# Maxima of an attention item in two halves, keyed scores 16 steps behind, and no prologue in a 12-stage decoder kernel

## The chip, the cores and the metric

One NeuronCore of a Trainium2 chip runs the whole program in one launch. The metric is the device time of that launch in microseconds (us). The engines are TensorE (PE in the profile, its weight loads PEld), VectorE (DVE), ScalarE (ACT), GpSimd (POOL) and SyncE (SP), which here only issues DMAs.

## The reference

Four decoder layers run over `x` of 8 sequences x 256 tokens x 128 features in float32. Each layer has three parts, each with a layer norm before it and a residual after it: `x = x + attn(ln(x))`, `x = x + xattn(ln(x), ctx)`, `x = x + ffn(ln(x))`. What matters here are the five attention parts that share one routine:

- L0a and L1a: causal self-attention of 16 heads of width 8, with rotary positions on queries and keys;
- L0x and L1x: cross-attention to `ctx` with a mask; L0x also multiplies each probability by a given matrix ("group prob") after the softmax;
- L3x: plain cross-attention.

Each computes `softmax(q k^T / sqrt(8)) v` per head and a projection. L0f, L1f and L2f are mixtures of 8 experts with a routed token each; L2a, L2x, L3a and L3f are other parts, which the change leaves as they are.

## The kernel before

`program` calls `start`, then one function per stage. `attention(core, sts)` is called three times: for the pair L0a and L0x, for L1a and L1x, and for L3x alone. Every stage ends with a barrier of all engines (`end_pass`).

**`start`** (from line 2087) loads the weights, `ctx`, `x`, fills the constant rows of the images in DRAM, zeroes `sorted_in` (8.8 MB of DRAM that L0f needs) from GpSimd's queue, turns `ctx`, and issues the expert weights of L0f. It is a block of its own, so that nothing of the attention group starts before all engines have left it.

**Items and slots.** An item is one sequence of one stage, so a pair has 16 items and L3x has 8. Item i's work is put at fixed slots: step number `16 * i + offset`. Each engine's program is written by one loop over the slots (`for n in SLOTS`), and within a slot in the fixed order of the `if` blocks. The queues are in order, so the offsets decide what stands behind what. Offsets modulo 16 say which slot of the running item j a step of another item falls in:

- statistics, aggregate, variance (DVE), Ln and Exp (ACT) and the normalisation (POOL, `normalise`, lines 486 to 497) of item j+3 are at slots 0, 1, 2, 3, 4 and 5;
- the transposition of x is at slot 10, the projections K and Q of item j+2 at slots 14 and 4, and V of item j at slot 8;
- `cut` (line 378) splits a float32 matrix into three bfloat16 parts. For item j+2 it stands on POOL at slot 1 for k and slot 7 for q (the first two items on DVE). A rotary item needs five operations (lines 383 to 389), another two (388 and 389);
- SP writes the parts to an image in DRAM and reads them back in another layout (`parts_out`, `stack_in`), which gives the tiles `Kst` and `Qm`;
- `scores` (line 653), one unit per slot, 16 per item, is followed by `row_max` on DVE (line 875). PE runs at most two units ahead of DVE;
- after all 16 maxima of an item `cut_max` (POOL, lines 505 to 508, slot 16), `turn_max` (PE, line 608, slot 18), a copy (ACT, slot 19) and two DMAs (SP, line 463, slot 20) put the maxima as extra rows into `Qm`;
- `keyed_scores` (line 673, with line 675 or 678 for masks) makes the scores once more, transposed and with the maximum subtracted, TLAG = 24 slots behind `scores`. ACT takes the exponential (line 769). For L0x the product with the group matrix is on POOL in 5 of 8 units (line 525) and on DVE in the others, at slot 25 on. `times_v` (line 703) takes four units at a time, at slots 2, 6, 10 and 14;
- choosing heads (`SEL`), dividing, transposing (`AT`, line 626), projecting (`Y`) and adding to X are at 45, 49 and 55. `Xb`, the residual with the bias, is made on POOL at offset 45 (slot 13, line 556).

At the start of each attention call DVE zeroes `Qm` (lines 924 and 925) and `vaug` (line 927) between the steps of the first item. In the pair L1a and L1x SP issues the experts' weights (2 x 2 MB, line 1402) before all else.

## Time and profile before

| | us |
|---|---|
| median of 3 runs (lowest to highest) | 1810.36 (1806.36 to 1817.83) |
| the profiled execution, its own time | 1812.71 |
| span of its profile | 1810.9 |
| first attention group, first statistics to last residual | 56.9 to 435.6 |
| second group | 561.6 to 901.2 |
| third group | 1483.8 to 1662.3 |

The time of the profiled execution is 1.8 us above its span. The page gives busy time by engine and by slices of the span, the timeline gives instructions in order with the idle time before them and who ended it, and the answer for a tile gives first and last start of the instructions that use it. The clock column PEclk is 1.0 at 2.4 GHz and 0.5 at 1.2 GHz. The three attention groups take 897 us of the 1811, and the block in front of the first takes 56.9.

### The profile page before, as it was taken

Reading aid. Unit: us, or ns where it says so; the run is one execution under the profiler, and the core shown is the slowest. Engines: PE = TensorE matmul, PEld = TensorE weight load, DVE = VectorE, ACT = ScalarE, POOL = GpSimd, SP = SyncE. Lnnn points to the kernel's source line nnn. Section 1 sums busy time; section 2 is a strip of 40 time slices with the busy share of each in tenths; the row PEclk is TensorE's granted clock in tenths of the full one; section 3 lists DMA queues with packets and bytes.
Section 4 is the critical chain, followed back from the end, with each engine's and each line's share of the span. In section 5 each row is a group of like instructions: output and inputs, shape, how many; then the busy total and the mean of one; then the engine's idle time right before and its main releaser. Section 6 shows DMA issues by size and latency. Waiting matters only on the chain. (4 is left out here: it accounts for less than half of the span.)

```text
span 1810.9 us, 30796 instructions
## 1 busy us (share of the span) xinstructions
PE 1278.4 (71%) x9105; PEld 805.9 (45%) x9105; DVE 1026.2 (57%) x4304; ACT 604.7 (33%) x1441; POOL 556.3 (31%) x931
## 2 busy tenths in 40 slices
PE   0289999995392799999739255645677765996686
PEld 0146555553291456555329133435644432553332
DVE  0478787764776777777267522456533346773432
ACT  0025554442040255556404112102232322664221
POOL 1256368873341544463034000004300003411000
PEclk9879999998596799999959655876878886998798
DMA  9633443300114334443011300001200004320000
GB/s 251 205 118 113 137 147 116 115 23 14 35 53 177 119 113 121 143 133 112 4 39 56 143 0 0 13 31 52 67 8 0 0 32 141 112 86 3 0 0 23
DMA packets 134311, 138.28 MB, mean 76 GB/s; under 512 B 11328, under 2 KB 106176, under 8 KB 133136
## 3 DMA queue, kind: packets, MB, share of 16 engines
q1 hardware_dynamic: 128208, 119.79, 21.5%
q0 software_dynamic: 5952, 16.68, 3.3%
q8 instruction: 70, 1.15, 0.3%
q14 instruction: 81, 0.66, 0.1%
HBM read 84.10 MB, written 49.70 MB: 74 GB/s over the span
## 5 line engine op out<-in xcount | busy, mean ns | idle before, releaser
L769 ACT ACTIVATE L0a_Pr<-PS 128x512 f32<-128x512 f32 (+1 forms) x256 | 137.1, 547 | 159.3 <-PE PS L678 94.2
L769 ACT ACTIVATE L1a_Pr<-PS 128x512 f32<-128x512 f32 (+1 forms) x256 | 136.2, 548 | 122.6 <-PE PS L675 65.0
L525 POOL TENSOR_TENSOR L0a_PG<-L0a_Pr,L0a_G 128x512 f32<-128x512 f32 x80 | 106.6, 1336 | 29.1 <-ACT L0a_Pr L769 17.1
L875 DVE CUSTOM_DVE_ANT_0 L1a_junk<-PS,L1a_neg 128x256 bf16<-128x256 f32 x256 | 94.7, 420 | 35.1 <-PE PS L653 34.9
L653 PE MATMUL PS<-L0a_Kst,L0a_Qm 128*128 128x256 bf16 (+1 forms) x512 | 94.7, 271 | 11.6 <-DVE L0a_mx L875 10.7
L653 PE MATMUL PS<-L1a_Kst,L1a_Qm 128*128 128x256 bf16 (+1 forms) x512 | 94.2, 270 | 11.6 <-DVE L1a_mx L875 10.6
L878 DVE TENSOR_REDUCE L3x_mx<-PS 128x2 f32<-128x512 f32 x128 | 83.7, 686 | 31.9 <-PE PS L653 31.5
L673 PE MATMUL PS<-L1a_Qm,L1a_Kst 128*128 128x512 bf16 (+1 forms) x256 | 91.0, 356 | 9.2 <-DMA L1a_Qm<-L1a_mT 6.0
L875 DVE CUSTOM_DVE_ANT_0 L1a_junk<-PS,causal_q 128x128 bf16<-128x128 f32 (+1 forms) x256 | 78.3, 352 | 30.2 <-PE PS L653 29.5
L875 DVE CUSTOM_DVE_ANT_0 L0a_junk<-PS,causal_q 128x128 bf16<-128x128 f32 (+1 forms) x256 | 78.3, 352 | 30.1 <-PE PS L653 29.4
L673 PE MATMUL PS<-L0a_Qm,L0a_Kst 128*128 128x512 bf16 (+1 forms) x256 | 90.8, 355 | 5.7 <-DMA L0a_Qm<-L0a_mT 2.9
L875 DVE CUSTOM_DVE_ANT_0 L0a_junk<-PS,L0a_neg 128x256 bf16<-128x256 f32 x192 | 72.8, 418 | 38.8 <-PE PS L653 38.2
L769 ACT ACTIVATE L3x_Pr<-PS 128x512 f32<-128x512 f32 x128 | 73.5, 603 | 46.2 <-PE PS L673 45.8
L675 PE MATMUL PS<-neg_k,ident_b 128*128 128x256 bf16 x256 | 70.1, 274 | 0.0
L653 PEld LDWEIGHTS PS<-L0a_Kst,L0a_Qm 128*128 128x128 bf16 x512 | 44.0, 102 | 57.0 <-DVE L0a_mx L875 32.4
L653 PEld LDWEIGHTS PS<-L1a_Kst,L1a_Qm 128*128 128x128 bf16 x512 | 43.7, 102 | 56.9 <-DVE L1a_mx L875 31.7
L1063 POOL MEMSET L2f_ends<- 128x4 f32 x2 | 0.1, 101 | 204.7 <-POOLq L1571 204.7
L703 PE MATMUL PS<-L1a_Pr,L1a_vaug 128*32 128x256 f32 (+1 forms) x1024 | 61.7, 358 | 0.2 <-ACT L1a_Pr L769 0.2
L653 PE MATMUL PS<-L3x_Kst,L3x_Qm 128*128 128x256 bf16 x256 | 51.9, 288 | 7.5 <-DVE L3x_mx L878 4.7
L673 PE MATMUL PS<-L3x_Qm,L3x_Kst 128*128 128x512 bf16 x128 | 48.8, 389 | 9.7 <-ACT L3x_Pr L769 5.1
L678 PE MATMUL PS<-L0a_neg,ident_b 128*128 128x512 bf16 x128 | 48.8, 381 | 0.0
L678 PE MATMUL PS<-L1a_neg,ident_b 128*128 128x512 bf16 x128 | 48.5, 379 | 0.0
(727 smaller groups left out, 3291.8 us busy)
## 6 DMA issues: line engine op xcount, KB each, us to landing
ffn_w_<-L_ffn SPq DMA_DIRECT2D x6, 2048.0 KB, 11.9
sorted_in<-zeros POOLq DMA_DIRECT2D x2, 4386.0 KB, 42.8
L0a_Kst<-k_image SPq DMA_DIRECT2D x64, 128.0 KB
L0a_Qm<-q_image SPq DMA_DIRECT2D x64, 128.0 KB
L1a_Kst<-k_image SPq DMA_DIRECT2D x64, 128.0 KB
L1a_Qm<-q_image SPq DMA_DIRECT2D x64, 128.0 KB
L3x_Kst<-k_image SPq DMA_DIRECT2D x32, 128.0 KB
L3x_Qm<-q_image SPq DMA_DIRECT2D x32, 128.0 KB
```

Of the source, the lines that this page charges most:

```text
L525: g.tensor_tensor(PG[:, V_ % GATED_RING, :].rearrange("p (h q) -> p h q", h=2), Pr[:, V_ % RING, :].rearrange("p (h q) -> p h q", h=2), G[ ...
L653: ins = mm(PS[:, bank, par * nk:(par + 1) * nk], Qm[:, buf, par, hp, tt * P:(tt + 1) * P], Kst[:, buf, hp, 0:nk], start=(par == 0), stop=T ...
L673: ins = mm(o, Kst[:, buf, hp, kt * P:(kt + 1) * P], Qm[:, buf, :, hp, q0:S], start=True, stop=True, **free)
L675: ins = mm(o[:, :, 0:P], core.ident_b[:, :], core.neg_k[:, :].unsqueeze(1).broadcast_to([P, 2, P]), start=False, stop=True, **free)
L678: ins = mm(o, core.ident_b[:, :], neg[:, buf, 1, kt].unsqueeze(1).broadcast_to([P, 2, S]), start=False, stop=True, **free)
L703: ins = mm(o, vaug[:, buf, half, kt, 4 * g + j, :], src[:, par * nq:(par + 1) * nq], start=(kt == 0 and half == 0), stop=True, **free)
L769: a(Pr[:, V_ % RING, 0:2 * nq], PS[:, T_BANK + v % 2, 0:2 * nq], ACT.Exp, scale=SCALE)\
L875: ins = v.tensor_tensor_reduce(junk[:, tt, par, 0:nk], scored[:, par], off, 1.0, LOWEST, ALU.add, ALU.max, mx[:, i % 2, tt, par, hp:hp + 1])
L878: ins = v.tensor_reduce(mx[:, i % 2, tt, :, hp:hp + 1], scored, AX, ALU.max)
L1063: nc.gpsimd.memset(ends[k][:, 0:E // 2], 0.0).then_inc(s["pads"], 1)
```

## The change

1. `start` is removed. Its loads are issued by SP at the head of the first attention call (`first_loads`): the part of `x` for the first two sequences, common weights, L0a's weights, the rest of `x`, the constant rows, `ctx`. The transposition of `ctx` is at slot -12 of the first group, the constant casts on DVE at slot -36.
2. `sorted_in` is zeroed in 8 parts, one per item at slot 5 on POOL's queue, and the experts' weights of L0f and L1f come one expert per item at slot 5 on SP's queue, where they were issued before the group's first item.
3. `Qm` and `vaug` live through the whole program and are zeroed once, at the start.
4. The statistics of the first three items of a group are made early (`LEAD`), with three buffers, and their K and Q steps are drawn together by 4 and 8 slots. Of item 0, the k stack is read back two slots ahead of the q stack.
5. The maxima of an item are handled in two halves: `cut_max` at slots 8 and 16, `turn_max` at 9 and 17, the copy at 10 and 18, the DMAs at 11 and 19. Operations and DMAs are twice as many at half the size.
6. TLAG is 16 where it was 24; V, SEL, AT, Y, XB and GATE_IN move with it (XB to slot 5, SEL to 5, AT to 8, Y to 11), and the two PSUM banks of these steps are dealt out anew.

```diff
-        self.zeros = sb("zeros", [P, 2 * (D + 1)])
+        self.zeros = sb("zeros", [P, D + 1])
+        self.Qm = sb("Qm", [P, DEPTH, 2, HP, S], BF16)
+        self.vaug = sb("vaug", [P, DEPTH, 2, TS, HP, 32])
...
-    EARLY = 2
+    RUNS = 3
...
     STATS, AGGR, VAR, LN, EXP, NORM = -48, -47, -46, -45, -44, -43
-    XT, K, Q, V, MT, SEL, AT, Y = -38, -34, -28, 8, 18, 45, 49, 55
-    K_CUT, Q_CUT, K_OUT, Q_OUT, MAX_CUT, MAX_IN = -31, -25, -27, -21, 16, 20
-    STACK_IN, FIRST_STACK_IN = (-13, -7), -20
-    MASK_IN, NEG, GATE_IN, XB = -23, -7, 4, 45
-    TLAG = 24
+    XT, K, Q, V, SEL, AT, Y = -38, -34, -28, 7, 37, 40, 43
+    MAX_CUT, MT, MAX_IN = (8, 16), (9, 17), (11, 19)
+    K_CUT, Q_CUT, K_OUT, Q_OUT = -31, -25, -27, -21
+    STACK_IN, FIRST_STACK_IN = (-13, -7), {"k": -22, "q": -20}
+    MASK_IN, NEG, GATE_IN, XB, FFN_IN, ZERO_IN = -23, -7, -4, 37, 5, 5
+    CONSTS, CTX = -36, -12
+    TLAG = 16
     PV_LAG = TLAG + 6
     SLOTS = range(STATS, PER * (N - 1) + Y + 2)
-    f_bank = lambda off: F_BANK + (off // 2) % 2
+    FILLED = {XT: 0, K: 0, SEL: 0, AT: 0, Q: 1, V: 1, Y: 1, MT[0]: 1, MT[1]: 1}
+    f_bank = lambda off: F_BANK + FILLED[off]
+    LEAD = {off: (0, 11, 20) for off in (STATS, AGGR, VAR, LN, EXP, NORM, XT, XT + 1)}
+    LEAD.update({off: (0, 4, 8) for k in (K, Q) for off in range(k, k + 8)})
+    def slot_of(i, off):
+        return PER * i + off - (LEAD[off][i] if i < 3 and off in LEAD else 0)
     def at(n, off):
-        i, r = divmod(n - off, PER)
-        return i if r == 0 and 0 <= i < N else None
+        return next((i for i in range(N) if slot_of(i, off) == n), None)
+    def before(n, off):
+        return sum(1 for i in range(N) if slot_of(i, off) < n)
...
-    def stack_slot(i, half):
-        return PER * i + (FIRST_STACK_IN if i < DEPTH else STACK_IN[half])
+    def stack_slot(i, half, what):
+        if i >= DEPTH:
+            return PER * i + STACK_IN[half]
+        return FIRST_STACK_IN[what] if i == 0 else PER * i + FIRST_STACK_IN["q"] - LEAD[Q][i]
+    cut_on_dve = lambda i, what: i == 0 or i == 1 and what == "k"
...
-        mrest = sb("mrest", [P, TS, 2, HP])
-        mpart = sb("mpart", [P, TS, 2, DH, HP], BF16)
-        mT = sb("mT", [P, S], BF16)
+        mrest = sb("mrest", [P, TS, 2, HP // 2])
+        mpart = sb("mpart", [P, TS, 2, 2, DH, HP // 2], BF16)
+        mT = sb("mT", [64, 2, S], BF16)
...
+                if first:
+                    first_loads(core, sp)
                 load_next_weights(core, sp)
-                if sts[0] == "L1a":
-                    load_ffn(core, sp, "L1")
-                sp.wait_ge(s["image_set"], 16 * 6)
...
+                    for half in range(2):
+                        i = at(n, MAX_IN[half])
                         if i is not None:
-                            if i >= DEPTH:
-                                sp.wait_ge(s["st_psum"], PER * (i - DEPTH) + 8 * (half + 1))
-                            if i == 0:
-                                sp.wait_ge(s["setup"], set_up)
-                            stack_in(i, half, "k")
-                            stack_in(i, half, "q")
-                    i = at(n, MAX_IN)
-                    if i is not None:
-                        sp.wait_ge(s["mT_ready"], i + 1)
-                        for par in range(2):
-                            sp.dma_start(Qm[64 * par + 56:64 * par + 64, i % DEPTH, par].rearrange("c p t -> c (p t)"),
-                                         mT[64 * par:64 * par + 64, :])\
-                                .then_inc(s[f"max_in{i % 2}"], 16)
+                            sp.wait_ge(s["mT_ready"], 2 * i + half + 1)
+                            for par in range(2):
+                                to = Qm[64 * par + 56:64 * par + 64, i % DEPTH, par, 4 * half:4 * half + 4]
+                                sp.dma_start(to.rearrange("c p t -> c (p t)"), mT[32 * par:32 * par + 32, half, :])\
+                                    .then_inc(s[f"max_in{i % 2}_{half}"], 16)
+                    i = at(n, FFN_IN)
+                    if i is not None and i < E and second:
+                        if first and i == 0:
+                            sp.wait_ge(s["ctx_psum"], 4)
+                        load_expert(core, sp, sts[0][:2], i)
...
+                if first:
+                    still = core.ffn[1][:, 0:S].bitcast(BF16).rearrange("p (k t) -> p k t", k=2)
+                    for k in range(2):
+                        g.memset(still[:, k, :], -float(k)).then_inc(s["still_set"], 1)
+                    g.memset(vaug[:, :, :, :, :, :], 0.0).then_inc(s["setup"], 1)
+                    g.memset(core.zeros[:, :], 0.0).then_inc(s["consts"], 1)
+                g.memset(mpart[:, :, :, :, NMAX:DH, :], 0.0).then_inc(s["setup"], 1)
...
-                def cut_max(i):
-                    pool.wait_ge(s["s_max"], PER * (i + 1))
+                def cut_max(i, half):
+                    pool.wait_ge(s["s_max"], PER * i + 8 * (half + 1))
                     if i > 0:
-                        pool.wait_ge(s["mT_psum"], i)
-                    hi, mid, lo = (mpart[:, :, :, k, :] for k in range(NMAX))
-                    top = mx[:, i % 2]
+                        pool.wait_ge(s["mT_psum"], 2 * (i - 1) + half + 1)
+                    hi, mid, lo = (mpart[:, :, half, :, k, :] for k in range(NMAX))
+                    top = mx[:, i % 2, :, :, 4 * half:4 * half + 4]
...
+                    for half in range(2):
+                        i = at(n, MAX_CUT[half])
+                        if i is not None:
+                            cut_max(i, half)
+                    i = at(n, ZERO_IN)
+                    if first and i is not None and i < ZERO_PARTS:
+                        if i == 0:
+                            pool.wait_ge(s["consts"], 2)
+                        some = SORTED_ROWS // ZERO_PARTS
+                        pool.dma_start(core.dram["sorted_in"][i * some:(i + 1) * some].rearrange("(p b) d -> p b d", p=P),
+                                       core.zeros[:, :].unsqueeze(1).broadcast_to([P, some // P, D + 1]))\
+                            .then_inc(s["rows_zero"], 16)
...
-                def turn_max(i, bank, n):
-                    pe.wait_ge(s["m_parts"], i + 1)
+                def turn_max(i, half, bank, n):
+                    pe.wait_ge(s["m_parts"], 2 * i + half + 1)
                     bank_empty(n, bank)
+                    if first and i == 0:
+                        pe.wait_ge(s["consts"], 2)
                     for t in range(TS):
-                        ins = tr(PS[:, bank, t * 64:t * 64 + 64].bitcast(BF16),
-                                 mpart[:, t].rearrange("p r c h -> p (r c h)"), core.ident_b[:, :])
+                        ins = tr(PS[0:64, bank, t * 64:t * 64 + 64].bitcast(BF16),
+                                 mpart[:, t, half].rearrange("p r c h -> p (r c h)"), core.ident_b[:, :])
...
-                    if v == 0:
-                        pe.wait_ge(s[f"max_in{i % 2}"], 32 * (i // 2 + 1))
+                    if v % 8 == 0:
+                        pe.wait_ge(s[f"max_in{i % 2}_{v // 8}"], 32 * (i // 2 + 1))
+                    if first and i == 0 and v == 0:
+                        pe.wait_ge(s["ctx_done"], 4)
...
+                if first:
+                    v.memset(Qm[0:64, :, 1], 0.0).then_inc(s["setup"], 1)
+                    v.memset(Qm[64:P, :, 0], 0.0).then_inc(s["setup"], 1)
...
-                    if n == VAR + 1:
-                        v.memset(Qm[0:64, :, 1], 0.0)
-                        v.memset(Qm[64:P, :, 0], 0.0).then_inc(s["setup"], 1)
-                    if n == K + 3:
-                        v.memset(vaug[:, :, :, :, :, :], 0.0).then_inc(s["setup"], 1)
...
-def load_ffn(core, eng, ly):
+def load_expert(core, eng, ly, e):
     for n in (0, 1):
-        eng.dma_start(core.ffn[n][:, :], core.dram[f"{ly}_ffn{n + 1}"]).then_inc(core.sem[f"ffn_w{ly[1]}"], 16)
+        cols = slice(e * F, (e + 1) * F)
+        eng.dma_start(core.ffn[n][:, cols], core.dram[f"{ly}_ffn{n + 1}"][:, cols]).then_inc(core.sem[f"ffn_w{ly[1]}"], 16)
...
+def first_loads(core, sp):
+    s = core.sem
+    tokens = lambda n: core.dram[n].rearrange("(t p) d -> p t d", p=P)
+    near = NSEQ * TS
+    sp.dma_start(core.X[:, 0:near, :], tokens("x")[:, 0:near, :]).then_inc(s["x_in"], 16)
+    sp.dma_start(core.W[:, :], core.dram["small_common"]).then_inc(s["w_in"], 16)
+    sp.dma_start(core.stage_W[0][:, 0:width(WEIGHTS[STAGES[0]])], core.dram[f"small_{STAGES[0]}"]).then_inc(s["first_w"], 16)
+    sp.dma_start(core.X[:, near:, :], tokens("x")[:, near:, :]).then_inc(s["x_rest"], 16)
+    still = core.ffn[1][:, 0:S].bitcast(BF16).rearrange("p (k t) -> p k t", k=2)
+    sp.wait_ge(s["still_set"], 2)
+    for k in range(2):
+        still_rows = lambda n: core.dram[f"{n}_image"][k, 6:8].rearrange("s r t -> r s t")
+        sp.dma_start(still_rows("k"), still[:, :, :]).then_inc(s["image_set"], 16)
+        for slot in range(2):
+            sp.dma_start(still_rows("q")[:, slot:slot + 1, :], still[:, 0:1, :]).then_inc(s["image_set"], 16)
+    sp.dma_start(core.ffn[0][:, 0:B * S].rearrange("p (t d) -> p t d", d=D), tokens("ctx")).then_inc(s["ctx_tok"], 16)
```

## Rows read from the trace of the kernel before

**Rows 1.** The page, busy time, share of the span and instructions of each engine.
```profile
PE 1278.4 (71%) x9105; PEld 805.9 (45%) x9105; DVE 1026.2 (57%) x4304; ACT 604.7 (33%) x1441; POOL 556.3 (31%) x931
```

**Rows 2.** Timeline, first 60 us: start, length, engine, line, tiles, idle before and releaser.
```profile
1.88 3.74 POOL L2121 DMA_DIRECT2D sorted_in<-zeros  x2 [0.32 <-POOL zeros L2117]
...
49.48 0.81 SPq L1402 DMA_DIRECT2D ffn_w_<-L_ffn  x2
...
56.93 0.49 DVE L909 BATCH_NORM_STATS2 L0a_st<-X 128x6 f32<-128x128 f32 x2 [50.79 <-PEq L2093]
```

**Rows 3.** By tile Qm, three groups: ns min/median/max, first to last start in us.
```profile
L653 PE MATMUL PS<-L0a_Kst,L0a_Qm x512: 216/273/421, 89.0 to 397.0; 128*128 128x256 bf16 x128, 128*128 128x128 bf16 x43
L673 PE MATMUL PS<-L0a_Qm,L0a_Kst x256: 272/379/634, 112.8 to 425.9; 128*128 128x512 bf16 x96, 128*128 128x256 bf16 x32
...
L653 PE MATMUL PS<-L1a_Kst,L1a_Qm x512: 216/273/421, 593.6 to 871.2; 128*128 128x256 bf16 x128, 128*128 128x128 bf16 x43
L673 PE MATMUL PS<-L1a_Qm,L1a_Kst x256: 272/379/634, 617.5 to 893.6; 128*128 128x512 bf16 x96, 128*128 128x256 bf16 x32
...
L653 PE MATMUL PS<-L3x_Kst,L3x_Qm x256: 269/273/421, 1510.0 to 1635.5; 128*128 128x256 bf16 x128
L673 PE MATMUL PS<-L3x_Qm,L3x_Kst x128: 379/379/634, 1532.4 to 1655.0; 128*128 128x512 bf16 x128
```

**Rows 4.** Timeline, starts of the second and third attention group.
```profile
561.57 0.49 DVE L909 BATCH_NORM_STATS2 L1a_st<-X 128x6 f32<-128x128 f32 x2 [3.10 <-PEq L1039]
...
563.11 2.62 DVE L924 MEMSET L1a_Qm<- 64x3072 uint32 x1 [0.57 <-issue]
...
571.34 2.62 DVE L927 MEMSET L1a_vaug<- 128x3072 f32 x1 [0.59 <-issue]
...
580.37 1.36 SPq L422 DMA_DIRECT2D L1a_Kst<-k_image  x2
...
1483.76 0.49 DVE L909 BATCH_NORM_STATS2 L3x_st<-X 128x6 f32<-128x128 f32 x2 [2.40 <-PEq L1694]
```

**Rows 5.** Timeline of POOL in one item of L0a.
```profile
159.06 0.19 POOL L488 TENSOR_TENSOR L0a_nsq<-L0a_r 128x2 f32<-128x2 f32 x1 [0.95 <-ACT L0a_r L787]
...
160.20 1.57 POOL L495 TENSOR_SCALAR L0a_xn<-X,L0a_mv,L0a_rstd 128x128 f32<-128x128 f32 x2
161.74 0.73 POOL L383 TENSOR_TENSOR L0a_qrot<-L0a_qrot 128x256 f32<-128x256 f32 x1
...
164.22 0.67 POOL L389 TENSOR_TENSOR L0a_qpart<-L0a_qrest,L0a_qpart 128x256 bf16<-128x256 f32 x1
164.85 0.86 POOL L556 TENSOR_TENSOR L0a_Xb<-X,stage_W 128x128 f32<-128x128 f32 x2
170.70 0.21 POOL L505 CAST L0a_mpart<-L0a_mx 128x32 bf16<-128x32 f32 x1 [4.98 <-DVE L0a_mx L875]
...
171.59 0.24 POOL L508 TENSOR_TENSOR L0a_mpart<-L0a_mrest,L0a_mpart 128x32 bf16<-128x32 f32 x1
```

**Rows 6.** Timeline of PE in the same item.
```profile
153.05 0.28 PE L653 MATMUL PS<-L0a_Kst,L0a_Qm 128*128 128x128 bf16 x2
...
162.67 0.27 PE L675 MATMUL PS<-neg_k,ident_b 128*128 128x256 bf16 x1
...
171.90 0.41 PE L626 MATMUL PS<-W,L0a_A 128*128 128x128 f32 x2 [0.49 <-DVE L0a_A L958]
```

**Rows 7.** Timeline of POOL and PE in two items of L0x.
```profile
283.06 0.21 POOL L505 CAST L0a_mpart<-L0a_mx 128x32 bf16<-128x32 f32 x1
...
309.58 0.21 POOL L505 CAST L0a_mpart<-L0a_mx 128x32 bf16<-128x32 f32 x1
...
323.39 0.64 PE L703 MATMUL PS<-L0a_PG,L0a_vaug 128*32 128x256 f32 x8 [2.19 <-POOL L0a_PG L525]
```

**Rows 8.** PE in L1x after a wait; then windows: busy us, PEclk, DMA share, GB/s.
```profile
735.69 0.61 PE L673 MATMUL PS<-L1a_Qm,L1a_Kst 128*128 128x512 bf16 x1 [3.16 <-DMA L1a_Qm<-L1a_mT]
...
735.00:740.00 5.00, 4.31 (x34) 2.90 (x35) 1.89 (x12) 1.79 (x3) 2.65 (x2) 0.66 0.42 113
```

More of the change, by code:

```diff
@@ L296, in attention @@
     S_BANK, T_BANK, O_BANK, F_BANK = 0, 2, 4, 6
+    first = core.at == 0
     any_masked = any(st in MASKED for st in sts)
@@ L450, in _ @@
                     for half in range(2):
-                        i = next((j for j in range(N) if stack_slot(j, half) == n), None)
-                        if i is not None:
-                            if i >= DEPTH:
-                                sp.wait_ge(s["st_psum"], PER * (i - DEPTH) + 8 * (half + 1))
-                            if i == 0:
-                                sp.wait_ge(s["setup"], set_up)
-                            stack_in(i, half, "k")
-                            stack_in(i, half, "q")
@@ L713, in _ @@
                 for n in SLOTS:
+                    if first and n == CTX:
+                        pe.wait_ge(s["ctx_tok"], 16)
+                        for k in range(4):
+                            for t in range(4):
+                                ins = tr(PS[:, T_BANK + k, t * P:(t + 1) * P], core.ffn[0][:, (4 * k + t) * D:(4 * k + t + 1) * D],
+                                         w("ident"))
+                            ins.then_inc(s["ctx_psum"], 1)
                     i, u = unit(n, 0)
@@ L734, in _ @@
                         project_v(i, f_bank(V), n)
-                    i = at(n, MT)
-                    if i is not None:
-                        turn_max(i, f_bank(MT), n)
+                    for half in range(2):
+                        i = at(n, MT[half])
+                        if i is not None:
+                            turn_max(i, half, f_bank(MT[half]), n)
                     i = at(n, SEL)
@@ L770, in exponentials @@
                         .then_inc(s["p_ready"], 1)
+                if first:
+                    nc.scalar.preload_act_table_set("natural_log_exp_and_others")
                 for n in SLOTS:
+                    if first and n == CTX + 1:
+                        for k in range(4):
+                            act_copy(core, act, core.ctxT[:, k * 512:(k + 1) * 512], PS[:, T_BANK + k, :], s["ctx_psum"], k + 1,
+                                     s["ctx_done"])
                     i, v = unit(n, TLAG)
@@ L799, in _ @@
                         first_part(i, "q", f_bank(Q))
[L800 to L805 removed]
+                    for half in range(2):
+                        i = at(n, MT[half] + 1)
+                        if i is not None:
+                            act.wait_ge(s["mT_psum"], 2 * i + half + 1)
+                            if i > 0:
+                                act.wait_ge(s[f"max_in{(i - 1) % 2}_{half}"], 32 * ((i - 1) // 2 + 1))
+                            a(mT[:, half, :], PS[0:64, f_bank(MT[half]), 0:P].bitcast(BF16), ACT.Copy).then_inc(s["mT_ready"], 1)
                     i = at(n, AT + 1)
@@ L850, in take_v @@
                         dve.wait_ge(s["pv_done"], 4 * (i - DEPTH + 1))
+                    if first and i == 0:
+                        dve.wait_ge(s["setup"], set_up)
                     halves = vaug[:, buf].rearrange("p a t h r -> p a (t h) r")
@@ L1428, in _ @@
                 load_next_weights(core, sp)
-                load_ffn(core, sp, "L2")
+                for e in range(E):
+                    load_expert(core, sp, "L2", e)
                 end_pass_sync(core, sp, "channel_attention")
@@ L2166, in program @@
         core = Core(nc, ctx, dram)
-        start(core)
         for core.at, st in enumerate(STAGES):
```

192 lines of the change are left out of this document (75 added, 117 removed).

## The prediction

> **What bounds the kernel now.** I read the page first, then the timeline of the first 100 us, the answers for the tile Qm, and then the timelines of POOL and PE inside single items. PE is the busiest engine [rows 1]. The start is idle time: DVE waits 50.79 us for the barrier at the end of the first block and begins at 56.93, while DMAs fill the queues and the experts' weights are issued at 49.48 [rows 2]. Scores begin at 89.0, 593.6 and 1510.0 in the three groups, keyed scores 24 slots later, and they end 28.9, 22.4 and 19.5 us after the last scores [rows 3]. Inside an item of L0a slot 0 of PE starts at 153.05 and the last matmul of slot 9 at 162.67. Slot 1 of the next item comes at 171.9 less a wait of 0.49 [rows 6], so an item is some 16.8 us. PE has few gaps in it, so what makes PE wait in its queue costs time.
>
> **The start (step 1, 2).** Before, scores start at 89.0 [rows 3]. After, DVE first has two memsets of Qm, 2.62 us each [rows 4], and its statistics start at about 6.6. The chain from statistics to scores is bounded by group two: 561.57 to 593.6, 32.0 us, with three memsets of 2.62 in DVE's queue [rows 3, 4]. Without them and with the next items' statistics out of the way, what ends last is SP. The k parts are ready some 10.5 us after the statistics (14.3 before, less three memsets and the steps between, plus a rotation of another item). Two image writes of three DMAs and eight reads of stacks at 0.6 to 0.7 us each (the row has two in 1.36) and two landings of about 2 us follow, one pair after the other because k is read back before q is written. That is 24 us. In the first group the image DMAs stand behind about 4 MB of loads, so I add 1 us: 6.6 + 24 = 31. **Gain 58 us.** The bounds are 47 (chain as in group two, 6.6 + 32 + 3 of queueing) and 62. The wait for x's second part on DVE, the constant casts and the turning of ctx lie in gaps of that chain. If the loads came late, all of it would move.
>
> **Starts of groups two and three (steps 2 to 4).** 32.0 becomes 24, so 8 us. Group three has 1483.76 to 1510.0, 26.2 us, with the short cuts [rows 3, 4]; there SP's chain gives 22, so 4 us. **Gain 12**, bounds 0 and 22 (all memsets of both).
>
> **The lag (step 6).** Eight slots of keyed scores alone leave each tail. The rows give 28.9 / 24 = 1.20, 22.4 / 24 = 0.93 and 19.5 / 24 = 0.81 us each [rows 3], so 9.6 + 7.5 + 6.5 = **24 us gain**. In the head eight slots then have both kinds of scores. The head's 24 slots last 23.8, 23.9 and 22.4 us [rows 3], 1.0 a slot, and a full slot of L0a is 16.8 / 16 = 1.05, so I take that at nothing; the bound is 8 x 0.3 in each group, 7 us.
>
> **The halves (step 5) and POOL's order.** This is the price. Four operations of `cut_max` take 170.70 to 171.8, 1.1 us, and at half the width I take the same, since small operations are 0.21 and 0.24 long [rows 5]. The first half stands at slot 8, behind all that POOL has at slots 5 and 7: `normalise` 159.06 to 161.77 (2.7 us), now Xb (0.86, moved from slot 13 to slot 5), and the q cut 161.74 to 164.89 (3.15) [rows 5]. `normalise` can't start before the Exp of slot 4, for which POOL waited 0.95 in that row. So the parts of half 0 are ready at 159.06 + 2.7 + 0.86 + 3.15 + 1.1 = 166.9. PE asks for them at the end of slot 9, 162.8 [rows 6]. PE stands 4.1 us, and behind it stand scores, keyed scores, the products with V and x's transposition of slot 10, and so DVE and ACT. Before, the request was at slot 18, two slots after the cut, and POOL was idle for 4.98 us ahead of it [rows 5].
> - L0a and L1a, running items 2 to 5: 4.1 less about 0.5 that the caught-up DVE gives back, 3.6. Item 1 has no Xb: 2.7. Items 6 and 7 have the short q cut (1.1): 1.6. Item 0 has only the normalisation: 0. That is 14.4 + 2.7 + 3.2 = 20 a group, **40 us**.
> - Half 1 is asked for in slot 1, about 0.6 us before it is ready, where PE now waits 0.49 for the A of the AT step [rows 6]; these cancel.
> - L0x: POOL also has the gate products, and PE already waits 2.19 us at slot 10 for that of slot 8 [rows 7]. An item with normalisation lasts 309.58 - 283.06 = 26.5 us [rows 7]. In front of PE's slot 10 come Xb (1.3 beside the gates, by my reading of the row's 0.86 as the lower bound), the cut (1.1), the scores of slot 10 (0.65) and, since half 1 stands behind the gate product of slot 0, some 2 us at slot 1. I take 5.6 for each of items 9 to 12, 1.5 for item 8 and 3 for each of 13 to 15: **33 us**, bounds 12 (only the cuts, 16 x 1.1 less what slack takes) and 45.
> - L1x and L3x have no gates and the short cut: 0 to 2.1 for each of 10 items, I take 1, less the 3.16 us wait for a maxima DMA [rows 8], which now has one slot more: **7 us**.
>
> **Small edits.** The eight zeroing parts move to POOL's slot 5. Two DMAs took 3.74 us to issue [rows 2], so a part is 0.9 (by rows) to 1.9 (by DMA), and 0.95 of idle time stands ahead of the normalisation [rows 5]; nothing, bound 8. If that idle time is gone, it adds to the stall of the same item. The doubled maxima DMAs are 0.65 us each on SP, which has room. The memsets of vaug and the small buffers on POOL at the start end before the first normalisation. Expert weights come 0.5 MB an item beside image DMAs: nothing, bound 4.
>
> **The clock.** After the 3.16 us wait the next 5 us ran at 0.66 of the full clock [rows 8]. At half clock for some 3.4 us of it, 1.7 us are lost. Of 14 stalls of about 4 us or more (5 and 5 in L0a and L1a, 4 in L0x) I let a third lose it: **8 us**. "TensorE: Matmul & The Clock Gate" of the Trainium skill (Part 1) says that the full clock is not a boost but what activity gives and idleness takes away, which speaks against this change. By it nearly each such stall would cost the clock, and the sum would be 16 us higher. The row agrees in kind: it shows the half level (1.2 GHz) entering the mean right after a wait.
>
> **The sum** against the profiled execution's 1812.7: gains 58 + 12 + 24 = 94; prices 40 + 33 + 7 + 8 = 88. That is 1807 in that execution, which lies 2.3 us over the median of the runs shown, so 1805.
>
> **Rivals.**
> 1. *The stalls are mostly taken up* (0.32). For it: PE's matmuls are pipelined, each stall lets ACT and DVE catch up, an item of 16.8 us has some 2 us of small gaps, and POOL's chain could start earlier than the row shows. Against it: POOL's queue is in order and its 7.8 us between Exp and parts are row values. At a third of the price (27 us and no clock): 1810 - 94 + 27 = 1743; at two thirds 1770. I put this case at 1765.
> 2. *The clock falls after nearly each stall* (0.22, slower). Place: slots 10 to 13 behind each wait for the first half. Price: 1.7 us for each of 14 long stalls and 8 shorter ones, 37 instead of 8, and with it PE gives back nothing of the caught-up DVE (0.5 x 12 = 6): 1805 + 29 + 6 = 1840. It decides if the mean clock of L0a's middle windows, 1.0 before, falls under about 0.9.
> 3. *The start is not as early* (0.08): the loads queue as before and scores begin at 45 to 50 instead of 31; 1820 to 1824, with the rest as forecast. Related: the change of order does nothing to the barrier's 50 us, which the diff excludes.
>
> **How the numbers follow.** Forecast 0.38, rivals 0.32, 0.22 and 0.08. 1% of 1810.36 is 18 us, the least that a measurement of this kernel tells from no change. The forecast's own range is 1785 to 1825: of its 0.38 some 0.08 is faster, 0.28 the same, 0.02 slower. Rival 1 is faster with nearly all of its 0.32, rival 2 slower with 0.19, the same with 0.01 and faster with 0.02 (if the start gives 62 and the tails more), rival 3 is 0.05 the same and 0.03 slower. So faster 0.42, same 0.34, slower 0.24. Cases of both signs hold much of the chance; the range reaches from two thirds absorbed to the clock rival: 1743 to 1842.
>
> **What would show it.** First scores at 29 to 34 us confirm the start; 24 us from the first statistics of group two to its scores the second term. In L0a, PE's wait ahead of line 608's successor for POOL's parts should be 3.5 to 4.5 us in items 1 to 5, with POOL busy from `normalise` to the cut without a gap, and the item at 20 us. L0x items should last 29 to 32 us. Scores to last keyed scores in the tail: 19 us in L0x and 15 in L1x. I am wrong if POOL reaches `cut_max` of slot 8 before PE ends slot 9, or if an item of L0a stays below 17.5 us; then the time is that of rival 1 or lower.

## The result and the profile after

The changed kernel takes 1959.6 us (median of 4 runs, 1950.0 to 1964.1) against 1811.1 for the kernel before (4 runs, 1806.4 to 1817.8): a ratio of 1.081, 95% interval 1.076 to 1.086, so 148 us slower. The profiled execution took 1949.99 us with a span of 1948.2; the sum below is made in the two spans, 1810.9 and 1948.2.

First the page of the changed kernel: busy time of the engines, the granted clock in 40 slices, and three groups with their idle time and what ended it.

```profile
PE 1329.0 (68%) x9185; PEld 822.5 (42%) x9185; DVE 1011.3 (52%) x4285; ACT 623.7 (32%) x1481; POOL 596.4 (31%) x1110
...
PEclk8688899999587699888895955586869985999698
...
L724 PE MATMUL PS<-Qm,L1a_Kst 128*128 128x512 bf16 (+1 forms) x256 | 98.8, 386 | 51.0 <-DMA Qm<-L1a_mT 49.5
L724 PE MATMUL PS<-Qm,L0a_Kst 128*128 128x512 bf16 (+1 forms) x256 | 96.8, 378 | 44.5 <-DMA Qm<-L0a_mT 43.1
```

Against [rows 1] PE has 50 us more busy time for nearly the same products (80 small matmuls more, of the halves): they ran at the half clock more often. But the two last lines are the news. Keyed scores (line 724) wait 92.6 us for the DMA that brings the maxima into Qm. On the page of the kernel before, the same wait was 8.9 us, and the prediction used one case of it, 3.16 us [rows 8]:

```profile
L673 PE MATMUL PS<-L1a_Qm,L1a_Kst 128*128 128x512 bf16 (+1 forms) x256 | 91.0, 356 | 9.2 <-DMA L1a_Qm<-L1a_mT 6.0
...
L673 PE MATMUL PS<-L0a_Qm,L0a_Kst 128*128 128x512 bf16 (+1 forms) x256 | 90.8, 355 | 5.7 <-DMA L0a_Qm<-L0a_mT 2.9
```

The tile Qm shows how the stretches moved, in the changed kernel:

```profile
L702 PE MATMUL PS<-L0a_Kst,Qm x512: 219/273/421, 33.0 to 453.6; 128*128 128x256 bf16 x128, 128*128 128x128 bf16 x43
...
L702 PE MATMUL PS<-L1a_Kst,Qm x512: 219/273/421, 638.7 to 1002.8; 128*128 128x256 bf16 x128, 128*128 128x128 bf16 x43
...
L724 PE MATMUL PS<-Qm,L0a_Kst x256: 272/379/634, 74.2 to 476.5; 128*128 128x512 bf16 x96, 128*128 128x256 bf16 x32
...
L724 PE MATMUL PS<-Qm,L1a_Kst x256: 272/379/634, 665.8 to 1017.9; 128*128 128x512 bf16 x96, 128*128 128x256 bf16 x32
...
L702 PE MATMUL PS<-L3x_Kst,Qm x256: 269/273/421, 1633.2 to 1778.7; 128*128 128x256 bf16 x128
...
L724 PE MATMUL PS<-Qm,L3x_Kst x128: 379/379/634, 1659.2 to 1792.1; 128*128 128x512 bf16 x128
```

With the first statistics and the last write of X of each group, read in the same way, the two spans split like this (us):

| stretch | before | after | difference | forecast |
|---|---|---|---|---|
| start to first scores | 89.0 | 33.0 | -56 | -58 |
| group 1, first scores to last X | 346.5 | 454.3 | +108 | about +50 |
| group 2, statistics to scores | 32.0 | 24.5 | -8 | -8 |
| group 2, first scores to last X | 307.6 | 386.3 | +79 | about +20 |
| group 3, statistics to scores | 26.2 | 22.8 | -3 | -4 |
| group 3, first scores to last X | 152.3 | 166.2 | +14 | about -5 |
| everything between and behind | 857.3 | 861.1 | +4 | 0 |

The starts came as forecast. The tails, last scores to last keyed scores, went from 28.9, 22.4 and 19.5 [rows 3] to 22.9, 15.1 and 13.4: 19 us of the 24. Nearly all that was missed lies inside the items. From the last keyed scores of group 2 to the first scores of group 3, work which the runs below hardly alter, it takes 607 to 622 us over the profiled executions of all kernels, so a few us mean nothing there.

**POOL's order, as predicted.** An item of L0a of the changed kernel in the timeline, the same stretch as [rows 5, 6] (start, length, engine, line); POOL first:

```profile
171.28 0.86 POOL L599 TENSOR_TENSOR L0a_Xb<-X,stage_W 128x128 f32<-128x128 f32 x2
172.11 0.72 POOL L403 TENSOR_TENSOR L0a_qrot<-L0a_qrot 128x256 f32<-128x256 f32 x1
...
174.58 0.67 POOL L409 TENSOR_TENSOR L0a_qpart<-L0a_qrest,L0a_qpart 128x256 bf16<-128x256 f32 x1
175.19 0.20 POOL L539 CAST L0a_mpart<-L0a_mx 128x16 bf16<-128x16 f32 x1
...
176.03 0.22 POOL L542 TENSOR_TENSOR L0a_mpart<-L0a_mrest,L0a_mpart 128x16 bf16<-128x16 f32 x1
```

PE in the same stretch:

```profile
172.58 0.38 PE L724 MATMUL PS<-Qm,L0a_Kst 128*128 128x512 bf16 x1
172.80 0.27 PE L726 MATMUL PS<-neg_k,ident_b 128*128 128x256 bf16 x1
176.30 0.42 PE L657 MATMUL PS<-ident_b,L0a_mpart 128*64 128x128 bf16 x2 [3.23 <-POOL L0a_mpart L542]
176.66 0.39 PE L702 MATMUL PS<-L0a_Kst,Qm 128*128 128x128 bf16 x2
176.84 0.63 PE L724 MATMUL PS<-Qm,L0a_Kst 128*128 128x512 bf16 x1
```

Xb, the q cut and `cut_max` follow one another without a gap, and PE stands 3.23 us for the parts. The same matmul takes 0.38 us ahead of the wait and 0.63 behind it: PE is at the half clock. The granted clock is 0.97 in 172.0 to 176.3 us and 0.57 in 176.3 to 180.0. In L1a the same wait is 1.94 us an item, and it is enough: the granted clock is 1.00 in 694.0 to 696.4, the wait ends at 698.38, and in 698.4 to 700.0 the clock is 0.50 and in 700 to 702 it is 0.57.

**SP's order, not predicted.** The same view of POOL in an item of L1x:

```profile
898.89 0.22 POOL L542 TENSOR_TENSOR L1a_mpart<-L1a_mrest,L1a_mpart 128x16 bf16<-128x16 f32 x1
899.20 3.93 POOL L551 TENSOR_SCALAR L1a_neg<-L1a_msk 128x512 bf16<-128x512 int32 x2
```

And of SP's queue beside it, then PE's next keyed scores:

```profile
892.54 1.46 SPq L433 DMA_DIRECT2D k_image<-L1a_kpart  x3
903.15 0.37 SPq L458 DMA_DIRECT2D L1a_msk<-mask1q  x1
...
904.14 1.29 SPq L441 DMA_DIRECT2D L1a_Kst<-k_image  x2
...
908.33 1.45 SPq L485 DMA_DIRECT2D Qm<-L1a_mT  x2
...
912.12 0.61 PE L724 MATMUL PS<-Qm,L1a_Kst 128*128 128x512 bf16 x1 [5.00 <-DMA Qm<-L1a_mT]
```

At slot 9 SP asks for the next masks, for which POOL must have used the last ones. POOL does so from 899.20 to 903.13, and SP stands from 894 to 903.15. Behind it, in SP's queue, stand two stack reads, the q image writes and, since the change, the maxima DMA of slot 11. It used to be at slot 20, which is slot 4 of the next item and 11 slots behind the mask wait; now it is 2 slots behind. It is issued at 908.33, and keyed scores begin at 912.1 after a wait of 5.00 us.

**Landings.** The DMA view of 105 to 235 us: queues with packets, MB and share; transfers with their count, size and us from issue to landing. First the kernel before:

```profile
q1 hardware_dynamic: 19672, 16.10, 41.0%
...
k_image<-L0a_kpart SPq DMA_DIRECT2D x8, 64.0 KB, 1.8
```

The changed kernel, with the two loads that moved in:

```profile
q1 hardware_dynamic: 16378, 15.23, 46.1%
q0 software_dynamic: 1575, 6.11, 31.0%
...
sorted_in<-zeros POOLq DMA_DIRECT2D x5, 1096.5 KB, 13.7
...
ffn_w_<-L_ffn SPq DMA_DIRECT2D x10, 256.0 KB, 11.1
...
k_image<-L0a_kpart SPq DMA_DIRECT2D x5, 64.0 KB, 12.2
```

A transfer of 64 KB that landed in 1.8 us takes 12.2. It is one of the three that write a k image; the one of 192 KB went from 2.1 us to 2.9, the one of 128 KB from 2.1 to 9.8. In item 0 the first maxima DMA is ready at 47.9 (ACT's copy), issued from 63.9 because SP stands at the stacks of items 1 and 2, whose images land late, and PE waits 21.04 us for it, at the start of item 1.

### The profile page after: what moved, and what is told of

It reads as the page before. It is cut to its first block and busy times, and to the rows that moved or that the text cites. A ratio compares the mean times of both kernels' runs of the same rounds, so it can differ in the third digit from the quotient of the medians.

```text
span 1948.2 us, 31472 instructions
## 1 busy us (share of the span) xinstructions
PE 1329.0 (68%) x9185; PEld 822.5 (42%) x9185; DVE 1011.3 (52%) x4285; ACT 623.7 (32%) x1481; POOL 596.4 (31%) x1110
## 5 line engine op out<-in xcount | busy, mean ns | idle before, releaser
L724 PE MATMUL PS<-Qm,L1a_Kst 128*128 128x512 bf16 (+1 forms) x256 | 98.8, 386 | 51.0 <-DMA Qm<-L1a_mT 49.5
L724 PE MATMUL PS<-Qm,L0a_Kst 128*128 128x512 bf16 (+1 forms) x256 | 96.8, 378 | 44.5 <-DMA Qm<-L0a_mT 43.1
L702 PE MATMUL PS<-L1a_Kst,Qm 128*128 128x256 bf16 (+1 forms) x512 | 99.6, 283 | 10.0 <-DMA Qm<-q_image 5.8
L702 PE MATMUL PS<-L0a_Kst,Qm 128*128 128x256 bf16 (+1 forms) x512 | 98.1, 279 | 10.3 <-DMA Qm<-q_image 6.7
L726 PE MATMUL PS<-neg_k,ident_b 128*128 128x256 bf16 x256 | 75.4, 294 | 0.0
L702 PEld LDWEIGHTS PS<-L1a_Kst,Qm 128*128 128x128 bf16 x512 | 44.9, 105 | 54.3 <-issue 22.6
L754 PE MATMUL PS<-L1a_Pr,vaug 128*32 128x256 f32 (+1 forms) x1024 | 67.2, 385 | 0.7 <-ACT L1a_Pr L828 0.7
L702 PEld LDWEIGHTS PS<-L0a_Kst,Qm 128*128 128x128 bf16 x512 | 45.2, 105 | 51.1 <-issue 19.6
L702 PE MATMUL PS<-L3x_Kst,Qm 128*128 128x256 bf16 x256 | 53.3, 295 | 10.4 <-DVE L3x_mx L946 6.5
L724 PE MATMUL PS<-Qm,L3x_Kst 128*128 128x512 bf16 x128 | 49.4, 390 | 9.2 <-DMA Qm<-L3x_mT 7.3
L724 PEld LDWEIGHTS PS<-Qm,L1a_Kst 128*128 128x128 bf16 x256 | 26.7, 104 | 63.2 <-DMA Qm<-L1a_mT 51.9
L729 PE MATMUL PS<-L1a_neg,ident_b 128*128 128x512 bf16 x128 | 52.7, 412 | 0.0
```

Of the source, the lines that this page charges most:

```text
L702: ins = mm(PS[:, bank, par * nk:(par + 1) * nk], Qm[:, buf, par, hp, tt * P:(tt + 1) * P], Kst[:, buf, hp, 0:nk], start=(par == 0), stop=T ...
L724: ins = mm(o, Kst[:, buf, hp, kt * P:(kt + 1) * P], Qm[:, buf, :, hp, q0:S], start=True, stop=True, **free)
L726: ins = mm(o[:, :, 0:P], core.ident_b[:, :], core.neg_k[:, :].unsqueeze(1).broadcast_to([P, 2, P]), start=False, stop=True, **free)
L729: ins = mm(o, core.ident_b[:, :], neg[:, buf, 1, kt].unsqueeze(1).broadcast_to([P, 2, S]), start=False, stop=True, **free)
L754: ins = mm(o, vaug[:, buf, half, kt, 4 * g + j, :], src[:, par * nq:(par + 1) * nq], start=(kt == 0 and half == 0), stop=True, **free)
```

## The experiments

Three theories. **Q**: order in in-order queues, POOL's (cut behind q cut) and SP's (maxima DMA behind the mask wait). **D**: the zeroing parts and expert loads make short transfers land late. **C**: the clock and the short lag as such. An item is counted in its group: items 0 to 7 of group 1 are L0a's, 8 to 15 L0x's, and so for L1a and L1x. The first four go from the changed kernel.

```
e1:  MASK_IN  -23 -> -20
e2:  Q_CUT    -25 -> -24;   XB  37 -> 41
e3:  items 8..15 instead of 0..7 for FFN_IN and ZERO_IN (i -= B)
e4:  TLAG 16 -> 24;  V, SEL, AT, Y, GATE_IN, XB, banks as in the kernel before
     MAX_CUT, MT, MAX_IN = (14, 16), (16, 18), (18, 20)
```

**Masks asked for later (e1).**

> One number of the changed kernel is altered: SP asks for the next masks three slots later (slot -20 instead of -23), behind the DMA of the first half's maxima instead of ahead of it. Theory Q (order in queues): in L1x SP waits up to 10 us for POOL's mask arithmetic with the maxima DMA standing behind it, and PE's keyed scores wait 4.8 to 5.9 us for that DMA; so L1x items fall from 25.5 us to about 20, L0x by 0 to 1, the rest by nothing: 1950 less 8 x 5 = 1910, 1900 to 1925. Theory D (DMA traffic: zeroing parts and experts' weights slow every landing): L1x has little of that traffic, nothing changes: 1950 +- 8. Theory C (what costs is the clock and the shorter lag as such): the wait moves elsewhere, 1940 to 1960.

1880.8 us (1.040, 1.034 to 1.046), 79 less than the change. What PE and SP waited for in 786 to 934 us (total, times, longest), the changed kernel first:

```profile
PE PS L724 <- DMA Qm<-L1a_mT: 29.8, 6, 6.9
...
SPq L458 <- POOL L1a_neg L551: 51.6, 6, 10.0
```

The same in e1:

```profile
PE PS L724 <- DMA Qm<-L1a_mT: 0.2, 1, 0.2
...
SPq L458 <- POOL L1a_neg L551: 2.7, 5, 0.6
```

The window's own line (busy us of PE, PEld, DVE, ACT, POOL; clock, DMA share, GB/s), changed kernel:

```profile
786.00:934.00 148.00, 117.54 (x936) 65.82 (x936) 85.31 (x458) 67.33 (x156) 61.04 (x123) 0.88 0.33 101
```

And e1:

```profile
786.00:934.00 148.00, 143.48 (x1233) 82.08 (x1232) 112.22 (x595) 88.61 (x197) 70.48 (x145) 1.00 0.38 118
```

Theory Q has the place, and was 30 us short in its number. Items 9 to 14 of group 2 (L1x) fall by 7.3 us each, not by 5: to the wait of about 5 us comes the clock, back from 0.88 to 1.00. Group 1 also gave back 11 us (the longest item of L0x, its second, went from 32.8 to 26.3).

**The q cut behind cut_max (e2).**

> Two numbers of the changed kernel are altered: POOL's q cut moves from slot 7 to slot 8, where it stands behind the first half's cut_max, and Xb from slot 37 to 41, behind it as well. Theory Q: PE's wait for POOL's parts (3.1 to 3.5 us an item in L0a and L1a, 2.5 to 4 in L0x) falls to under 1 us, and the half clock after it goes with it; L0a items 22.3 -> 18.5, L1a 20.3 -> 17.3, L0x 30.6 -> 28, L1x about 1 less: 1950 - 22 - 20 - 16 - 8 = about 1885, 1870 to 1905. Theory D: PE's wait moves to the maxima DMA, L0a items stay over 21 and the time at 1930 to 1950 except for L1a. Theory C: as theory Q for the waits, but items of L0a stay at half clock in their first slots and above 20 us.

1919.3 us (1.060, 1.053 to 1.067), 40 less. Below the waits of PE in L0a (100 to 220 us), the changed kernel:

```profile
PE PS L657 <- POOL L0a_mpart L542: 14.2, 6, 3.6
PE PS L724 <- DMA Qm<-L0a_mT: 9.4, 4, 4.9
```

The same in e2:

```profile
PE PS L724 <- DMA Qm<-L0a_mT: 28.7, 6, 7.0
PE PS L657 <- POOL L0a_mpart L542: 0.8, 2, 0.4
```

The wait for POOL is gone, and in L0a it is now one for the maxima DMA: theory D holds there. The mean of items 2 to 5 hides it: they last 17.0, 26.0, 16.9 and 25.4 us, so every second one meets a late landing and the others are free of both costs. In L1a, without zeroing parts, items fall from 19.5 to 16.9 as theory Q says. In L1x they rise by 0.9 us where 1 less was expected. Neither theory alone gives 1919.

**The loads later (e3).**

> The zeroing parts and the expert loads are issued in items 8 to 15 of their group instead of 0 to 7; nothing else differs. Theory D: item 1 (42.5 us, with PE waiting 21 us for the first maxima DMA, which took 10 us to land) falls to about 25, items 2 to 7 of L0a lose 1 to 2 us each, L0x gains 1.3 us of POOL issue in each: 1950 - 17 - 9 + 8 = 1932, 1915 to 1942. Theory Q: item 1 falls a little (SP still stands at the stacks of items 1 and 2), the 3.1 us waits stay, L0x is longer by POOL's 1.3 us: 1945 to 1958.

1934.2 us (1.069, 1.063 to 1.075), 25 less: item 1 falls from 42.1 to 26.5 as theory D says, items 2 to 5 only by 1.0 us each (the POOL wait holds them: 12.6 us in 100 to 220), and L0x rises by 1.3. Over its eight items L0a gives back 37 us (201.9 to 164.6), and L0x, where the loads now are, takes 12 (218.6 to 230.5).

**Lag and slots as before (e4).**

> The changed kernel with its start, loads and halves, but the lag and the slots of the steady part as before: keyed scores 24 slots behind, first half cut at slot 14, second at 16, turned at 16 and 18, maxima DMAs at 18 and 20, Xb, SEL, AT, Y and the banks as before. Theory Q: both queue stalls are gone, items last what they did before (16.7, 24, 16.7, 17.9, 16.3), and the gain of the starts (56 + 7.5 + 3.4) stays: 1811 - 67 = 1744, 1738 to 1760. Theory D: the first 220 us keep their traffic, item 0 to 7 of L0a lose 15 to 35 us to it: 1760 to 1780. Theory C in the form that the clock falls because of the denser start: over 1790.

1834.1 us (1.015, 1.009 to 1.021), 125 less than the change and still more than before. The numbers of theories Q (1744) and D (1760 to 1780) are missed. Theory C had said "over 1790", which fits, but not its reason: the mean granted clock of the profiled execution is 0.837, in the spread of the kernel before (0.825 to 0.855), and what is left over has a place. L1a is back (17.3), but L0a has 30.4 us in item 1 and 24 to 26 in items 6 and 7. In L0x and L1x PE waited 10.4 and 10.3 us in all for the bank in which I had put the first half's transposition. So the maxima go back into one piece:

```
e5:  the changed kernel with
-    MAX_CUT, MT, MAX_IN = (8, 16), (9, 17), (11, 19);  TLAG = 16
+    MT, MAX_CUT, MAX_IN = 18, 16, 20;                  TLAG = 24
     mrest, mpart, mT, cut_max, turn_max, V, SEL, AT, Y, GATE_IN, XB,
     banks and waits as in the kernel before
e6:  also FFN_IN and the zeroing parts in items 8..15,
     the parts issued by SP at slot 13 instead of by POOL at slot 5
e7:  the changed kernel with e1, e2 and e6's loads (lag 16, halves)
```

> The changed kernel with the maxima of an item handled in one piece again, the lag of 24 and all slots and banks of the steady part as before; the start, the statistics together, the long-lived buffers and the loads in parts stay as changed. The kernel with lag 24 and two halves took 1826.5 us in its profiled execution, with L0x items of 23.7 to 28.5 us and L1x items of 20.5, where PE waited at the turning of the first half for the bank that DVE reads k from (10.4 us in L0x, 6.3 in L1x). Theory Q: those waits were of my placing of the first half; whole maxima bring L0x to 25 and L1x to 17.9: 1826 - 28 = 1800, 1792 to 1808. Theory D: L0a items 1 to 7 keep 155 us against 116 before, since the zeroing parts and expert loads are still there; the same 1800, and item 6 and 7 stay at 24. Against both: items back at 16.8 in L0a would mean that the halves caused them, and 1765.

> The same with the zeroing parts and the expert loads issued in items 8 to 15 of the group instead of 0 to 7, the zeroing parts from SP at slot 13 instead of from POOL at slot 5. Theory D: L0a items 2 to 7 fall to 16.7, item 1 to about 20; in L0x SP's issue is off the path and its DMA share has room: 1800 - 40 = 1760, 1748 to 1772. Theory Q alone: the stall of item 1 stays at 30 us and only the landings change: 1785 to 1795.

> The changed kernel with lag 16 and halves, and all three repairs together: masks asked for behind the maxima DMA, q cut and Xb behind the first half's cut_max, zeroing parts (from SP) and expert loads in items 8 to 15. If the three costs are separate: L0a items 2 to 7 at 17, item 1 at 27, L0x 28, L1a 17, L1x 19, L3x 17: 1950 - 72 - 41 - 24 and 15 more where q cut and loads together free L0a: about 1800, 1785 to 1815. If they share one stall (each repair only uncovers the next): 1840 to 1870.

| | us | ratio to before | item 1 | L0a 2-5 | L0x 10-14 | L1a 2-6 | L1x 9-14 |
|---|---|---|---|---|---|---|---|
| before | 1811 | | 15.6 | 16.6 | 24.0 | 16.8 | 18.2 |
| change | 1959.6 | 1.081 | 42.1 | 22.2 | 28.7 | 19.5 | 26.2 |
| e1 | 1880.8 | 1.040 | 40.3 | 22.3 | 28.7 | 19.6 | 18.9 |
| e2 | 1919.3 | 1.060 | 36.4 | 21.3 | 27.2 | 16.9 | 27.1 |
| e3 | 1934.2 | 1.069 | 26.5 | 21.3 | 30.0 | 19.2 | 26.5 |
| e4 | 1834.1 | 1.015 (1.009 to 1.021) | 30.4 | 18.6 | 25.9 | 17.3 | 19.8 |
| e5 | 1837.7 | 1.013 (1.007 to 1.018) | 31.1 | 27.7 | 24.3 | 16.8 | 18.1 |
| e6 | 1770.4 | 0.975 (0.969 to 0.981) | 15.9 | 16.6 | 26.2 | 16.8 | 18.3 |
| e7 | 1803.1 | 0.995 (0.991 to 0.999) | 23.6 | 16.9 | 27.2 | 16.7 | 18.9 |

(Columns: us per item between first scores, one profiled execution each.) e5 and e6 differ in the loads alone and by 67 us. e5 was expected at 1800; its L0a items take 27.7 us, not 24. e7, with all three repairs, took 1803 where about 1800 was expected. The three costs are separate: the repairs give 79, 40 and 25 us one by one, 144 in sum, and 156 together. Repairing them leaves a kernel with lag 16 and halves 33 us slower than one with whole maxima and lag 24 (e6).

Most of these 33 us are a fourth cost, in item 1 of every group: 23.6, 24.6 and 23.7 us in e7 against 15.9, 16.1 and 14.9 in e6, 25 us in all. The start of the second group in e7, ACT's copy, SP's queue and PE:

```profile
576.01 0.38 ACT L873 ACTIVATE L1a_mT<-PS 64x256 bf16<-64x256 bf16 x1 [10.12 <-PE PS L659]
...
577.66 1.22 SPq L441 DMA_DIRECT2D L1a_Kst<-k_image  x2
...
582.63 11.15 SPq L485 DMA_DIRECT2D Qm<-L1a_mT  x4
...
588.27 0.61 PE L726 MATMUL PS<-Qm,L1a_Kst 128*128 128x512 bf16 x1 [7.13 <-DMA Qm<-L1a_mT]
```

The first half's maxima of item 0 are ready at 576.4, but the stack reads of items 1 and 2 stand ahead of their DMA in SP's queue, which issues it at 582.63, and PE waits 7.13 us. The same wait is 6.9 us in group 1 and 6.7 in group 3. With whole maxima and the lag of 24 it is gone: in e6 the wait at that place is 0.3 us. It is SP's order again; no run moves this DMA alone, so this cause is read from the traces and not tested. So steps 5 and 6 of the change bring nothing here: the 19 us of the tails are lost in the items 1, in L0x and in the third group.

**Which load (e8, e9), and where to put them (e10, e11).** From e6, one kind of load goes back to items 0 to 7, or goes to the end of the group:

```
e8:   zeroing parts as changed (POOL, slot 5, items 0..7), experts in 8..15
e9:   experts in items 0..7, zeroing parts by SP in items 8..15
e10:  by SP: parts at slots 5, 7, 9, 21, 23, 25, 27, 29 of item 15,
      experts at slots 31 to 38
e11:  parts as in e10, experts in items 0..7
```

> Whole maxima and lag 24; the experts' weights come in items 8 to 15, but the zeroing parts (1.1 MB each, from POOL's queue at slot 5) stay in items 0 to 7 as changed. With both early the kernel took 1837.7 us and its L0a items 27 us; with both late 1770.4 and 16.7. If the zeroing parts are what makes the maxima DMA land late (theory DZ): L0a items 2 to 7 at 23 to 27, the time 1815 to 1835. If the expert loads are (DE): 16.7 to 18 and 1765 to 1780. If it takes both together: 18 to 22 and 1780 to 1805.

> The other half of the pair: the expert loads (0.5 MB an item, in SP's queue) stay in items 0 to 7, the zeroing parts come in items 8 to 15 from SP. DZ: L0a items 16.7 to 18, 1765 to 1780. DE: 23 to 27, 1815 to 1835. Both together: 18 to 22.

> Whole maxima and lag 24; three zeroing parts stand behind the maxima DMA of item 14, five behind that of item 15, then the eight expert loads, all from SP in the last slots of a group, when no stacks are read any more. The kernel with both in items 8 to 15 took 1770.4 us; its L0x items 8 to 15 last 195 us against 178 in the kernel before. Theory D: they fall to 180, the rest stays, and the loads are done before the first scatter of the expert block: 1770 - 15 = 1755, 1745 to 1765. Against it: if the first scatter or the experts' first block waits for these loads, 1770 to 1790.

> Whole maxima and lag 24; expert loads in items 0 to 7 as changed, where they cost nothing measurable (1771.0 against 1770.4 us), and the zeroing parts three behind the maxima DMA of item 14 and five behind that of item 15. With both kinds of loads at the end L0x items 8 to 15 lasted 178.7 us, but the expert block began later and the total was 1771.6. Theory: what came later there was the weights' 4 MB behind the zeroing parts; without it the block starts as before: 1771 - 12 = 1759, 1750 to 1766. Against it: if the zeroing parts alone make the expert block wait, 1768 to 1774.

e8 1830.6 us (1.007, 1.003 to 1.011), e9 1771.0 (0.974, 0.966 to 0.982): it is the zeroing parts, the experts' weights cost nothing that these times show. Against e6, which differs from e8 in the zeroing parts alone, L0a's eight items last 210 us for 132, and L0x, freed of the parts, 177 for 197. e10 1771.6 (0.974, 0.966 to 0.982), where 1745 to 1765 was expected: L0x falls to 24.3 as expected, but the block behind the group ends later. Scores of group 1 end 20 us earlier than in e6 (343.1 against 362.7), scores of group 2 begin 2 us later (554.1 against 552.1). e11 **1759.6** (0.969, 0.964 to 0.975) as expected, the lowest median, though its interval touches those of e6, e9 and e10: the change's start without its halves and its lag, and with the zeroing parts behind the last maxima DMAs.

**Queue or place (e12 to e14).** Only the zeroing parts of e8 are moved: by SP at slot 13, by POOL at slot 13, by SP at slot 5.

> Whole maxima, lag 24, expert loads in items 8 to 15, and the eight zeroing parts in items 0 to 7 as in the kernel that took 1830.6 us, but issued by SP at slot 13 instead of by POOL at slot 5. If the burst of 1.1 MB itself makes the small transfers behind it land late (burst): the k parts land in 8 to 12 us again, L0a items at 23 to 27, 1815 to 1835. If POOL's queue, or its place just before the image writes, is what does it (queue): k parts land in 2 to 4 us, L0a items at 17 to 19, 1770 to 1790.

> Zeroing parts in items 0 to 7 from POOL's queue, at slot 13 instead of slot 5; all else as in the kernel of 1830.6 us. Place: the burst of 11 to 12 us no longer meets the maxima DMA and the k image writes; 1770 to 1785. Queue: POOL's transfers hold back the others wherever they start; k parts land in 8 us and more, 1810 to 1835.

> Zeroing parts in items 0 to 7 from SP's queue, at slot 5 instead of slot 13; all else as in the kernel of 1774.2 us. Place: they stand behind the k image writes and the maxima DMA of slots 4 and 5 in SP's queue but start within 2 us of them; 1800 to 1835. Queue: SP's transfers go in order, so those ahead land first; 1770 to 1785.

e12 1774.2 (0.978, 0.973 to 0.983), e13 1781.4 (0.984, 0.979 to 0.990), e14 1778.2 (0.982, 0.976 to 0.988). The DMA view of 80 to 180 us in e8:

```profile
sorted_in<-zeros POOLq DMA_DIRECT2D x4, 1096.5 KB, 12.4
...
k_image<-L0a_kpart SPq DMA_DIRECT2D x4, 64.0 KB, 9.4
```

And in e13:

```profile
sorted_in<-zeros POOLq DMA_DIRECT2D x6, 1096.5 KB, 12.5
...
k_image<-L0a_kpart SPq DMA_DIRECT2D x6, 64.0 KB, 2.0
```

Both moves take most of it away: L0a's eight items last 210 us in e8, 148, 154 and 152 in e12, e13 and e14, and 132 in e6. So neither POOL's queue nor the bytes do it alone, and POOL's issue of 1.27 us does not either, as e13 still has it. What costs 50 us is a burst that starts just ahead of the transfers on which PE waits next. In e8 POOL issues it at 113.59, SP the maxima DMA at 113.90 and the k image at 115.35, and keyed scores begin at 125.67 after a wait of 8.70 us. In e14 the burst stands behind those transfers in SP's own queue; in e13 it starts 2 to 4 us after the k image's issue, and it is the q image's writes that land late there (9.8 us for 64 KB, 7.1 in e8), at little cost. Whether it would cost as much just ahead of them in SP's own queue is not shown: no run has it there.

## Why the prediction was wrong

- **Start, steps 1 and 2, and the second and third starts: right.** 33.0 instead of 31; 24.5 where 24 was said; 22.8 where 22 was.
- **Tails: right in kind**, 19 us instead of 24.
- **POOL's order in L0a, L1a and L0x: right in mechanism and place, not in size.** PE's wait is 3.1 to 3.6 us in L0a's items 2 to 5 and 1.94 in L1a's (4.1 forecast for both). The items are 22.2 and 20.3 us (20 forecast): in L1a the right number is partly luck, as half of it is the clock (0.92 over these items, 1.00 in e2). L0x items 9 to 12 last 30.6 to 32.8 us and 13 and 14 less, 26.7 and 24.8 (29 to 32 forecast). The terms given for L0x add up to 5.05 us an item and not to 5.6, a slip of 2 us in the sum. e2 takes the wait away by moving the cut.
- **"L1x and L3x have no gates and the short cut ... I take 1": the step that failed in group 2.** L1x items grew by 8.0 us. Their price was read from POOL alone; the DMA of the half was moved past SP's mask wait, and that queue was not gone through. "The doubled maxima DMAs are 0.65 us each on SP, which has room" counts SP's busy time, where its waits decide. e1 shows it: 79 us in all, and L1x's eight items last 147.9 us in it, for 199.7 in the changed kernel and 147.0 before. The item 1 of each group pays for the same omission, behind the stack reads.
- **"The eight zeroing parts ... nothing, bound 8" and "Expert weights ... nothing, bound 4": the step that failed in group 1.** The experts' weights were rightly nothing. The zeroing parts cost 60 us in the kernel with whole maxima (e8 against e6, 1830.6 and 1770.4); in the changed kernel, where POOL's wait holds the same items, moving both loads gives back 37 us in L0a and 25 in all (e3). I priced their issue on POOL (1.27 us now) and not what they do to the landings behind them, where before the same bytes left ahead of all scores [rows 2].
- **The clock (8 us): too little.** The profile's mean in 105 to 235 us is 0.86, where before it was 0.98; in L1x 0.88 against e1's 1.00. Rival 2's sign (under 0.9) is there, and its end, slower, too, but not its price: it takes 37 us for 22 stalls, and there were many more of them, with causes that it did not name. A wait of 1.94 us halves the clock as well, and there were many of that length. The clock is the smaller half: of 7.3 us an item in L1x some 5 are the wait and about 2 follow it.

The forecast of 1807 in this execution missed 1950 by 143 us, and 131 of them lie in the prices. From first to last scores L0a lasts 72 us longer than before (20 forecast), L0x 41 (33), L1a 34 (20), L1x 53 and L3x 20 (7 together): 219 us against 88 with the clock's 8. The gains are 86 where 94 was said, and 4 lie between the groups. Of this the runs give back nearly all of L1x's 53 (e1), 37 of L0a's 72 (e3), and the growth of L1a's items 2 to 5 (16.9 us each in e2, 17.0 before). L3x, which the forecast had at 1 us an item, has 12 of its 20 in items 0 and 1. How the rest divides between the waits and the clock the runs don't separate: each repair also changes the others.

## What to carry to other kernels

When a transfer is moved to an earlier slot, write down for its queue what it now stands behind and what that waits for; a queue that is idle most of the time can still be the one that ends last. A filler transfer is free only if it starts behind the short ones of its moment: the same 8.8 MB cost 60 us at one slot of POOL, and 3 to 11 eight slots later or in SP's queue, both against a place in items 8 to 15 that itself costs some 11 us more than the group's end (e9 and e11). And judge a change by parts: here the early start alone, with its loads well placed, gives 1759.6 us against 1811 (e11), which the halves, the lag and one badly placed transfer had buried.
